# A graph network's first layer: each finished block is multiplied inside its own group

## The reference, cut to what matters

```python
h = relu(layernorm(x))
feat = einsum('ni,rhid->rnhd', h, conv_weights)          # 8 relations x 4 heads x 64
e = leaky_relu(el[type, src] + er[type, dst], 0.2)
alpha = softmax of e over the edges of each dst
x = x + segment_sum(alpha * feat[type, src], dst) + h_bias
h = relu(layernorm(x))
h_all = einsum('ni,rio->nro', h, W)                      # W from comp and basis
agg = segment_sum(h_all[src, type], dst)
y = gelu(agg + h @ loop_w + bias + h)
x = x + layernorm(y) * gamma + beta
```

## Time and profile before

| | us |
|---|---|
| timed runs, median (lowest to highest) | 2781.35 (2780.27 to 2787.69) |
| profiled execution, its time | 2775.95 |
| its span, first to last instruction | 2774.0 |
| layer 0's gathers | about 220 to 1468 |
| between the layers, to the first gather of layer 1 | to 1548.6 |
| layer 1's gathers, the last issued | to 2757.0 |

### The profile page before, as it was taken

One profiled execution on the slowest core, in us unless ns is written; L12 is line 12 of the kernel. 1 busy time (PEld: TensorE's weight loads), 2 busy tenths in 40 slices (PEclk: granted clock), 3 DMA queues, 4 the chain that ended last, 5 costly groups with the idle time before them and its releaser, 6 DMA issues.

```text
span 2774.0 us, 26393 instructions
## 1 busy us (share of the span) xinstructions
PE 1935.9 (70%) x8092; PEld 1437.4 (52%) x8092; DVE 1523.4 (55%) x3167; ACT 675.4 (24%) x1247; POOL 2017.6 (73%) x2138
## 2 busy tenths in 40 slices
PE   7993567788888888787888556565656565656555
PEld 6982355555655555565555344444444444444444
DVE  7764677787778777877876323323332333333233
ACT  4754333444343434434432100000000000000001
POOL 5946777777777777777774577777777777777775
PEclk9996678889888988888889877767676868686776
DMA  8557555566665656665653533333333333333333
GB/s 237 214 192 222 146 148 166 168 170 181 179 171 166 185 167 172 176 183 165 171 161 90 161 105 105 105 111 105 111 104 112 110 106 110 106 111 109 107 110 93
DMA packets 168504, 403.11 MB, mean 145 GB/s; under 512 B 49741, under 2 KB 75820, under 8 KB 160682
## 3 DMA queue, kind: packets, MB, share of 16 engines
q0 software_dynamic: 95312, 261.58, 35.1%
q1 hardware_dynamic: 73050, 139.85, 14.4%
HBM read 325.41 MB, written 75.86 MB: 145 GB/s over the span
## 4 chain that ended last, share of the span: by engine, by line
POOL 53%; issue 18%; PE 15%; DVE 10%; DMA 2%; ACT 1%; DVEq 0%; POOLq 0%; ACTq 0%; SPq 0%
POOL Z L843 53%; PE PB L1838 5%; PE PB L1886 4%; PE PB L2002 3%; DVE Z L1382 3%; DVE ACC L1354 2%; DMA Z<-tab,KI 2%; PE PB L1966 1%; POOL Z L789 0%; PE PB L2007 0%; DVE ERM L1363 0%; ACT L1630 0%; DVEq L1330 0%; PE PB L2005 0%; DVE FW L1409 0%
## 5 line engine op out<-in xcount | busy, mean ns | idle before, releaser
L843 POOL DMA_INDIRECT Z<-tab,KI x1963 | 1860.9, 948 | 662.7 <-issue 591.0
L1886 PE MATMUL PB<-Z,OHZ 128*128 128x260 f32 (+1 forms) x3926 | 1198.6, 469 | 517.3 <-DMA Z<-tab,KI 386.3
L1886 PEld LDWEIGHTS PB<-Z,OHZ 128*128 128x128 f32 x3926 | 911.1, 240 | 751.1 <-DMA Z<-tab,KI 407.9
L1354 DVE TENSOR_TENSOR ACC<-ACC,PB 128x260 f32 (+1 forms) x997 | 421.8, 423 | 846.9 <-PE PB L1886 824.4
L1382 DVE TENSOR_TENSOR Z<-Z,PB 128x2048 f32<-128x2048 f32 (+1 forms) x125 | 284.1, 2273 | 0.1
L2002 PE MATMUL PB<-w,ht 128*128 128x512 f32 x480 | 270.8, 728 | 1.8 <-ACT ht L1756 1.8
L1966 PE MATMUL PB<-pick,ERM 128*128 128x16 f32 (+1 forms) x504 | 111.7, 372 | 170.8 <-DVE ERM L1363 170.8
L1966 PEld LDWEIGHTS PB<-pick,ERM 128*128 128x128 f32 (+1 forms) x504 | 108.3, 326 | 183.8 <-DVE ERM L1363 183.8
L1818 ACT ACTIVATE ACC<-ACC 128x256 f32<-128x256 f32 x30 | 10.4, 406 | 775.9 <-DVE ACC L1354 775.9
L2002 PEld LDWEIGHTS PB<-w,ht 128*128 128x128 f32 x480 | 112.0, 240 | 138.4 <-issue 135.8
L1716 ACT ACTIVATE OHZ<-OHZ,kid 128x4096 bf16<-128x4096 bf16 (+1 forms) x32 | 115.7, 3616 | 217.0 <-DMA OHZ<-dlt 217.0
(11 more groups left out here) (336 smaller groups left out, 1564.1 us busy)
## 6 DMA issues: line engine op xcount, KB each, us to landing
OHZ<-dlt SPq DMA_DIRECT2D x31, 1024.0 KB
Z<-tab,KI POOLq DMA_INDIRECT x1963, 2.8
tab<-st SPq DMA_DIRECT2D x120, 256.0 KB, 3.1
tab<-Z SPq DMA_DIRECT2D x24, 1040.0 KB, 3.9
TD<-typ SPq DMA_DIRECT2D x31, 256.0 KB
tab<-Z SPq DMA_DIRECT2D x5, 1024.0 KB, 8.3
xn<-xb SPq DMA_DIRECT2D x30, 128.0 KB, 2.3
X<-xn SPq DMA_DIRECT2D x6, 640.0 KB, 9.4
```

The source lines that it names most:

```text
L843: pool.indirect_dma_start(to, None, tab, at).then_inc(d_fe[g % 2][part(g, k) * layer], 16)
L1354: dv.tensor_tensor(a, a, bank(done + i)[:, 0:width], ALU.add).wait_op(*previous, "sem-ge").then_inc(*o.of(s_add))
L1886: last = pe.matmul(p, OH[:, slot, k + i, :], rows_, start=(i == 0), stop=(i == n - 1))
```

## The change

- TensorE, in iteration g, for blocks 0 to 26 (LATE = 27): `flip_block(r)` and the four quarters come behind the group's fourth pair, then `select(g+1)`, then the loop product (`own_product_of`), a wait until ScalarE has moved it, then pairs 4 and 5 of the same group (`early`). The flip goes to PB[1], the quarters to PB[0], PB[6], PB[7], PB[1], the loop product to PB[0], the pairs' own banks; each waits for the add that frees its bank. The rest of the late pairs is cut anew among the steps of the next group: 6 to 7, 8, 9 to 12, 13 to 15.
- VectorE: `finish(r)` is a generator: first half ahead of the second scaling of the group, second half (reciprocal and shift) behind the three adds that follow.
- ScalarE: block r is normed and its flip copied at the end of iteration g; its quarters and loop product are moved in iteration g+1 behind `turned`, ahead of `stage`.
- SyncE stores block r's own table rows in iteration g, behind the load of block r+2.
- GpSimd: the first gather of a group waits for four pairs, the fifth for s_es.
- Behind the loop: blocks 27 to 29 have a buffer each for the flipped block and a bank each for the loop product; the three loop products come after the last quarter. The lists' transpositions stand between the blocks, and VectorE casts two of them to KI.

```diff
-        def quarter_bank(j):
-            return PB[2 + j % 2]
+        LATE = finished_in(NG - 1)
+        def flip_bank(r):
+            return PB[3 if r >= LATE else 1]
+        def quarter_bank(r, j):
+            return PB[2 + j % 2 if r >= LATE else (0, 6, 7, 1)[j]]
+        def own_bank(r):
+            return PB[2 + r - LATE if r >= LATE else 0]
...
@@ sync @@
-                if 0 <= r and g < NG - 1:
+                if 0 <= r < LATE:
                     store_block(r)
-                    if r:
-                        store_table(r - 1)
                     load_block(r + 2)
+                    store_table(r)
...
@@ gpsimd, fetch @@
                         if k == 0:
+                            pool.wait_ge(s_pair, min(pair_no(g - 2, 4), pair_no(g - 1, 0)))
+                        elif k == 4:
                             pool.wait_ge(s_es, g)
...
-            pool.wait_ge(s_kt, VISITS + 4)
-            pool.tensor_copy(KI[:, :], TDF).then_inc(*o.of(s_loc))
...
@@ vector @@
+                norm = finish(finished_in(g)) if finished_in(g) >= 0 else iter(())
+                if g + 1 < NG:
+                    next(norm, None)
                 for c in range(8, n, 8):
                     scale_rows(g, c)
...
+                    if c == 8 and g + 1 < NG:
+                        next(norm, None)
...
-                if finished_in(g) >= 0:
-                    finish(finished_in(g))
+            next(norm, None)
             for q in range(added_in_turn(NG - 1), GROUPS[NG - 1][1] // 2):
                 add(pair_no(NG - 1, q), ROW0, 0)
-            finish(NB - 2)
-            finish(NB - 1)
+                if q == added_in_turn(NG - 1):
+                    next(norm, None)
+            for r in range(LATE + 1, NB):
+                for _ in finish(r):
+                    pass
+            for i in range(2):
+                dv.wait_ge(s_pt, VISITS + i + 1)
+                dv.tensor_copy(KI[:, 512 * i:512 * i + 512], PB[6 + i][:, :]).then_inc(*o.of(s_ki))
...
@@ scalar, loop @@
                     turned(g + 1)
+                r = finished_in(g - 1)
+                if r >= 0:
+                    for j in range(4):
+                        move_quarter(r, j)
+                    move_own(r)
+                if g + 1 < NG:
                     stage(g + 1)
...
+                r = finished_in(g)
+                if r >= 0:
+                    normed(r)
+                    move_flipped(r)
...
@@ tensor @@
             def flip_block(r):
                 pe.wait_ge(s_h, NB + r + 1)
-                if r:
+                if r < LATE:
+                    pe.wait_ge(s_add, pair_no(r + 4, 1))
+                elif r > LATE:
                     pe.wait_ge(s_ev, moved(r - 1, 3))
...
                 for j in range(4):
-                    if j > 1:
+                    if r < LATE and j < 3:
+                        pe.wait_ge(s_add, pair_no(r + 4, j + 2))
+                    if r >= LATE and j > 1:
                         pe.wait_ge(s_ev, moved(r, j - 2))
...
+            def own_product_of(r):
+                h, to = flipped(r), own_bank(r)
+                pe.wait_ge(s_ev, moved(r, 0) if r < LATE else moved(NB - 1, 3))
...
-                late(g - 1, 4, cuts(g)[0])
+                late(g - 1, early(g - 1), 8)
                 pe.wait_ge(s_pk, g + 1)
...
-                late(g - 1, *cuts(g)[0:2])
+                late(g - 1, 8, 9)
                 pe.wait_ge(s_cf, g + 1)
...
-                late(g - 1, *cuts(g)[1:3])
+                late(g - 1, 9, 13)
                 pe.wait_ge(s_xr, g + 1)
...
-                late(g - 1, cuts(g)[2], 16)
+                late(g - 1, 13, 16)
...
                 late(g, 3, 4)
+                r = finished_in(g)
+                if 0 <= r < LATE:
+                    flip_block(r)
+                    block_products(r)
                 if g + 1 < NG:
                     select(g + 1)
-                r = finished_in(g)
-                if r > 0:
-                    block_products(r - 1)
-                if r >= 0 and g + 1 < NG:
-                    flip_block(r)
+                if 0 <= r < LATE:
+                    own_product_of(r)
+                    pe.wait_ge(s_own, r + 1)
+                if g + 1 < NG:
+                    late(g, 4, early(g))
             late(NG - 1, 4, 16)
-            for r in range(finished_in(NG - 1), NB):
-                flip_block(r)
-                block_products(r)
+            flip_block(LATE)
+            block_products(LATE)
+            flip_block(LATE + 1)
+            pe.wait_ge(s_loc, 4)
+            pe.wait_ge(s_add, NPAIR)
+            turn_back(lambda t: ERM[:, 128 * t:128 * t + 128], (PB[6], PB[7]))
+            block_products(LATE + 1)
+            flip_block(LATE + 2)
+            turn_back(lambda t: TD[:, t, :], (PB[0], PB[1]))
+            block_products(LATE + 2)
+            for r in range(LATE, NB):
+                own_product_of(r)
```

More of the change, by code:

```diff
@@ L186, in program @@
         QQ = sb("QQ", [128, 129])
-        FW = sb("FW", [128, 128])
-        BW = sb("BW", [128, 128])
-        MX = sb("MX", [128, 128])
-        ZR = sb("ZR", [128, 128])
+        FBW = sb("FBW", [128, 2, 128])
+        FW, BW = FBW[:, 0, :], FBW[:, 1, :]
+        MXZ = sb("MXZ", [128, 2, 128])
+        MX, ZR = MXZ[:, 0, :], MXZ[:, 1, :]
         EX = sb("EX", [128, 128])
+        HTL = HT, FBW, MXZ
         PK = sb("PK", [128, 2])
@@ L438, in cuts, with early @@
             return (6, 10, 14) if g == NG - 1 else (5, 8, 11)
+        def early(g):
+            return 6 if 0 < g < NG - 1 else 4
         def landed(layer, g, k):
@@ L723, in _ @@
                 sp.dma_start(rows[:, i, :], t.rearrange("(o n) -> o n", o=1).to_broadcast([128, D])).then_inc(d_rows, 16)
-            last = finished_in(NG - 1)
-            store_table(last - 1)
-            store_block(last)
-            load_block(last + 2)
-            store_block(last + 1)
-            store_table(last)
-            store_block(last + 2)
-            store_table(last + 1)
-            store_table(last + 2)
+            store_block(LATE)
+            load_block(LATE + 2)
+            store_block(LATE + 1)
+            store_table(LATE)
+            store_block(LATE + 2)
+            store_table(LATE + 1)
+            store_table(LATE + 2)
             for i in range(2):
@@ L1483, in finish @@
                 s = r % 2
+                no = FIN + r
                 a = ACC[:, ROW0 * r:ROW0 * r + D].rearrange("p (h d) -> p h d", h=4)
@@ L1503, in finish @@
                 dv.bn_aggr(mv[:, r, :], st6[:, r, :]).then_inc(*o.of())
-                norm_scale(r, r + 1, FIN + r)
+                dv.wait_ge(*o.last())
+                dv.tensor_scalar(ve[:, r:r + 1], mv[:, r:r + 1, 1], 1e-5, None, ALU.add).then_inc(*o.of(s_ve))
+                yield
+                dv.wait_ge(s_sd, no)
+                dv.reciprocal(rs[:, r:r + 1], sd[:, r:r + 1]).then_inc(*o.of())
+                dv.wait_ge(*o.last())
+                dv.scalar_tensor_tensor(nmr[:, r:r + 1], mv[:, r:r + 1, 0], -1.0, rs[:, r:r + 1], ALU.mult,
+                                        ALU.mult).then_inc(*o.of(s_nm))
             lanes, shift, gamma = PB[5][:, 384:512], PB[0][:, 0:256], PB[5][:, 0:256]
@@ L1737, in move_quarter @@
                     ac.wait_ge(d_st[j], 16 * r)
-                ac.activation(ST1[:, j, :], quarter_bank(j)[:, :], ACT.Copy).then_inc(*o.of(s_ev))
+                ac.activation(ST1[:, j, :], quarter_bank(r, j)[:, :], ACT.Copy).then_inc(*o.of(s_ev))
             def move_own(r):
-                ac.wait_ge(s_mm, product_of(r, 4))
-                ac.activation(ACC[:, ROW0 * r:ROW0 * r + D], PB[2][:, 0:D], ACT.Copy).then_inc(*o.of(s_own))
+                ac.wait_ge(s_mm, own_product(r))
+                ac.activation(ACC[:, ROW0 * r:ROW0 * r + D], own_bank(r)[:, 0:D], ACT.Copy).then_inc(*o.of(s_own))
             def normed(r):
@@ L1755, in move_flipped @@
                 ac.wait_ge(s_tr, NB + r + 1)
-                ac.activation(HT[:, :, :].rearrange("p c n -> p (c n)"), PB[3][:, 0:256], ACT.Copy).then_inc(*o.of(s_ht))
+                ac.activation(flipped(r)[:, :, :].rearrange("p c n -> p (c n)"), flip_bank(r)[:, 0:256], ACT.Copy).then_inc(*o.of(s_ht))
             turned(0)
@@ L1789, in _ @@
                 ac.activation(EX[0:R, :], ZR[0:R, :], ACT.Exp).then_inc(*o.of(s_xr))
-            last = finished_in(NG - 1)
-            for j in range(4):
-                move_quarter(last - 1, j)
-            move_own(last - 1)
-            normed(last)
-            ac.wait_ge(s_oh, batch_no(NG - 1, G))
-            for i in range(2):
-                ac.wait_ge(s_pt, VISITS + i + 1)
-                ac.activation(DL[:, 512 * i:512 * i + 512], PB[2 + i][:, :], ACT.Copy).then_inc(*o.of(s_kt))
-            for i in range(2):
-                ac.wait_ge(s_pt, VISITS + i + 3)
-                ac.activation(TDF[:, 512 * i:512 * i + 512], PB[4 + i][:, :], ACT.Copy).then_inc(*o.of(s_kt))
```

(11 more changed lines are left out.)

66 lines of the change are left out of this document (24 added, 42 removed).

## The result

| | kernel before | changed kernel |
|---|---|---|
| median, 11 runs each (us) | 2782.43 | 2791.29 |
| lowest to highest | 2780.27 to 2787.69 | 2787.73 to 2795.25 |
| profiled execution: time, span | 2775.95, 2774.0 | 2790.63, 2789.0 |
| mean granted clock of TensorE | 0.808 | 0.812 |

The ratio is 1.0029, with a 95% interval of 1.0020 to 1.0037: the change costs 0.3%, 8.9 us at the medians and 14.7 us between the two profiled executions. The prediction was 2793.

What follows compares the result with a forecast made beforehand. GpSimd's gathers in layers 0 and 1 and the stretch between bound the kernel; -11.0 us behind the loop and +23 in it, +12 on the timed median 2781.35, gave 2793. Own range 2784 to 2803, overall 2768 to 2804.

Steps and rivals of the forecast that it cites:

- Part 1: Behind the loop, up to layer 1's first gather: a stretch shorter by 11.0 us, bounds 7 and 13.
- Block 26's 9 us: Behind the loop: block 26's quarters and loop product, together 9.0 us, leave the stretch for its group in the loop.
- the wait of 7.35: Behind the loop: VectorE's wait of 7.35 us at 1502.16 goes, of which it can use 6.9.
- Part 2: Inside a loop group: TensorE's round becomes 40.9 us, above GpSimd's 40.06, costing 23 us over 27 groups.
- the third rival: Clock also halved behind the loop's selection, slowing loop product, pairs 4 and 5; in half the groups: +40, 2821, chance 0.08.
- The margin at full clock: In a loop group: TensorE has 1.5 us to spare at full clock, a round of 38.5 us.
- The clock's weight: Loop quarters: half clock stays in most groups and costs 2.4 us each, against the skill's rule of under 1%.
- The loop's sum: In the loop: 0.85 us lost in each of 27 groups, 23 us in all, bounds 0 and 35.
- One sign named in the prediction: In the loop: VectorE's first step of a group waits no longer for the gathers; before, 129.8 us in 32 groups.
- The pace holds: Loop: clock cost under 1.5 us per group, so GpSimd never waits; only the gain behind the loop: 2770 us, chance 0.30.
- In part: TensorE late in some groups, 5 to 15 us, or behind the loop only VectorE's wait gained: 2779, chance 0.12.
- The wait at the fifth gather: Layer 0's fifth gather of a group waits for the selection; excluded, since met at 1224.4, gather at about 1232.

Runs made afterwards that it cites:

- one pair moved: Changed kernel with one late pair moved behind the transposition of the exponentials; 0.9838, 0.9796 and 0.9797 of the kernel before, all at the second level.
- two pairs: Changed kernel with two late pairs moved behind the transposition of the exponentials; 2780.89 us, 1.0011 of the kernel before, at the first level.
- the fillers: Changed kernel with 12 TensorE matmuls of unread result ahead of each flip in the loop; 1.0256 and 1.0273 of the kernel before, second level.

## Why the prediction was right

**Part 1, behind the loop: -11.0 forecast, -10.5 measured** (-13.1 at the second level). Block 26's 9 us and the wait of 7.35 are gone; the longest wait of an add there is 2.02 us. The last three products start 9.03 and 8.94 us apart, 9.3 forecast, 10.01 before. From the start of block 29's quarters to layer 1's first gather it is 10.59 us, 10.70 before, as the prediction had it.

**Part 2, one round of TensorE: 40.9 forecast, 40.97 measured.** From the transposition of line 2071 to the quarters 23.6 forecast (1190.49 to 1214.1), measured 1191.48 - (1208.60 - 40.97) = 23.85. Quarters with the clock 9.3, measured 9.46 to the selection's start. Pairs 4 and 5: 1.9, measured 1.86. Between them two terms were off and cancelled. The selection was put at 3.4 and took 1.8: the 3.59 of the earlier trace rows had the half clock in it, which I took for the operation's own time. The loop product with its evacuation was put at 2.6 and took 4.02 (1202.72 to 1206.74): 1.4 us more, at half speed. That is the mechanism of the third rival, to which I gave 0.08 and half of the groups. It came in 16 of the 21 rounds that I read, and in the other five the second stretch of half clock stood over the pairs of the next group; its 1.4 us replaced the 1.6 us of the selection, which the rival's sum had not counted.

This is more than a matter of two sizes. The step "the half clock of the quarters alone makes TensorE the bound" doesn't hold with the measured parts: 40.97 less the 1.4 us of the loop product is 39.6, an estimate from these rows, and that is under GpSimd's 40.06. The margin at full clock wasn't 1.5 us but about 2.9 to 3.1. The quarters' 2.4 us would have fitted into it; with the second stretch they didn't. So the forecast of the round, and with it that of the time, was right by luck in this part: a selection counted too slow stood in for a loop product counted too fast. That TensorE would be the bound, and GpSimd wait for it at the seventeenth gather, was right.

**The clock's weight.** The quarters of the loop's 25 blocks in the 1018 us of the earlier trace rows took 238.45 us, 9.54 for sixteen, 7.03 behind the loop. The idle 3.05 us ahead of the flip, and 0.5 behind it (4.1 forecast) was enough to keep the half clock in every group, as the row at 1486.92 had suggested. The Trainium skill (TensorE: Matmul & The Clock Gate, "What's actually happening") puts the ramp's penalty, for modelling, under 1% of a typical kernel's span; it says so of the matmuls at a kernel's start. The trace doesn't agree for this kernel, where the half clock comes back in every group: 2.5 us in 25 groups are 63 us, 2.2% of 2789, in the quarters alone. And what decides isn't the share but the place: 2.4 and 1.4 us of it in a round whose margin was about 3.

**The loop's sum: +23 forecast, +23.45 measured** up to line 2071 of the last group, of it 19.6 by way of 40.86 us between the first gathers of the groups 5 to 31 (40.10 before), and most of the rest in the last group, where TensorE is 1.8 us later behind VectorE than it was. The mean is under 40.97 because the first of these groups still came 40.1 to 40.5 us apart. One sign named in the prediction didn't come: VectorE's first step waits longer for the gathers, 190.5 us in all against 129.8. The last one starts 4.5 to 5.2 us ahead of that step in most groups, in place of 2.8 to 3.6, now that the stores run beside them; no run at this level moved the stores alone, so their part in it isn't shown. TensorE's lateness covered it.

**Rivals.** "The pace holds" needed a mean clock cost under 1.5 us, by the measured parts under about 3; it was 2.4 in the quarters and 1.4 in the loop product or the pairs behind it. "In part" fell with it. The wait at the fifth gather that I had excluded is absent at the first level and 6.4 us long at the second, where it does bind: the exclusion rested on the measured margin of this level, not on the order of the work.

**The median.** I put the difference of the profiled executions, +12, on the median. It was +14.7 between the executions, with 2.9 of it in layer 1, and +8.9 at the medians: the execution profiled before was 6.5 us under its median, that of after within 0.7 of its own.

**Open.** Whether one pair moved would beat both kernels at the first level: its neighbour with two pairs is level with the kernel before there. What the clock is worth by itself at that level, since the fillers ran only at the second. And what makes the second level.

## What to carry to other kernels

When a change makes a loop of several engines tight on TensorE, don't add up its round at one clock: take each operation's time with the clock that its row had, and ask where the half clock may move: with the idle time, and to places that have none ahead of them. Work taken off such a round may be given back by the clock, so read whole rounds in the trace (length, busy time, granted clock) and not only the step that was edited. A margin that decides should be larger than all stretches at half clock in a round cost: here about 3 us stood against 3.8.

## What the hardware showed that I had not expected

- Rounds of the kernel with two pairs moved come in two kinds, with a few between: 40.9 to 41.1 us at a granted clock of 0.83 ten times running, and 38.7 to 40.1 at 0.91, with TensorE busy 35.5 and 32.5 to 33.0 us for the same matmuls. Taking 0.5 us off the way to the flip left the first kind's length as it was (40.96 in the changed kernel).
- The granted clock also falls behind a busy stretch. From 1197.00 to 1203.36 in the changed kernel it is 1.00 and TensorE is busy 6.36 of 6.36 us, with the last quarters and the selection; from 1203.36 to 1206.77 it is 0.50.
- The sixteen matmuls of the selection, 16 columns each, take 3.59 us at half clock and 1.85 at full; of the scores, 24 take 0.86 us at full clock and 1.49 at half.
- At the second level fillers and flips are shown 0.70 us or a multiple of it apart behind a burst of 24 scores, and a pair's result reached VectorE 16.2 us after its matmuls are shown to end. Both kernels take a quarter longer in all there: a group of layer 0 takes 56.4 us before and 58.0 after the change in place of 40.1 and 41.0, layer 1's gathers 1369 in place of 1208. The same chip served at both levels.
